# Down projection of a quantised feed-forward block: every block of sums stays in its PSUM bank and is rescaled there

## The chip, the cores and the metric

The kernel runs on one core of a Trainium2 chip. The metric is the device time of one execution in microseconds (us). Names used below: PE is TensorE (PEld its weight loads), DVE is VectorE, ACT is ScalarE, POOL is GpSimd, SP is the SyncE queue that issues most DMAs.

## The reference, cut to what matters

A gated layer: a linear attention block, whose result is added to x, and then a feed-forward block with 4-bit weights, whose result is added again. x has 32 batches of 64 rows of 512 numbers, so 2048 rows. Only the feed-forward block is touched:

```python
# per group of 128 rows of a weight matrix: w[k,n] = q[k,n]*s[g,n] - (z[g,n]+1)*s[g,n],  g = k // 128
Wg, Wu = dequant(gate...), dequant(up...)      # 512 x 1376
Wd = dequant(down...)                          # 1376 x 512: 11 groups, the last of 96 rows
gate, up = x2 @ Wg, x2 @ Wu
inter = gate * sigmoid(gate) * up              # 2048 x 1376
out = (inter @ Wd).astype(float16)
x = x + tanh(g_ffn[0]) * out
```

The weight of one group is an integer (q - z - 1, held in the tile `d_int`) times a scale that depends on the group and the output column.

## The kernel before, in words

**Stages.** The attention block works through 16 pairs of batches in a software pipeline; in its last passes the integers of the three weight matrices are unpacked into SBUF. A drain of the pipeline follows, in which the scales are transposed (`scale_T`, `d_scale_T`) and the rows are normalised for the feed-forward block. Then comes the feed-forward block, on which the change lies. It is written out as 44 units (`UNITS`): 4 chunks of 512 rows (`CHUNKS`) times 11 blocks of 128 intermediate features (`IT`). Data lie transposed: features on partitions, 512 rows along the free axis.

**One pass n of the loop over units, on PE.** Eight jobs. Each job is first `gate_up(n, job)`: two fp16 matmuls (L1395, L1396) of one weight group against the high and the low part of x, into one of three banks in turn (`gu_bank`); a job cannot start before the bank of three jobs earlier has been read. Behind it each job does one piece of the down projection of unit n-2: jobs 0 to 3 `high_product`, jobs 4 to 7 `low_product`, one for each of the four blocks of 128 output columns (`nt`), each block in a PSUM bank of its own (`z_bank`). The intermediate is split into `in_hi` and `in_lo`, so a block takes one matmul with each (L1419, L1431).

**The four blocks of the down projection differ.** Blocks 0, 1 and 2 multiply by the integers, so the sum of each unit must be multiplied by its group's scale and added to a running sum in SBUF (`yT`). Block 2 is done by DVE in one instruction (`add_sum`, L1839; L1834 for a chunk's first unit). Blocks 0 and 1 take ACT to scale (`scaled`, L880) and POOL to add (`add_sum`, L614). Block 3 (`PLAIN`) multiplies by dequantised weights, split into `wd_hi` and `wd_lo`, and its sums stay in the bank through the 11 units; it takes three matmuls for each unit (L1416, L1417, L1428), and at the chunk's end ACT copies it out (`plain_sum`). Its weights are made in the drain: a broadcast DMA (`d_scale`, L418), a POOL product (L574), an ACT copy (L833), a POOL difference (L581).

**The other engines in pass n**, in the order of their queues. DVE: the block-2 sum of unit n-3, then six `add_group` (L1800; three for gate, three for up; each scales a bank and adds it into `acc`, so the second and third of a half read what the one before wrote). ACT: `open_sum(n, 0)` (L855, first group of gate), `high_part(n-1)` (L870), `open_sum(n, 1)` (first group of up), `scaled(n-2, 0)`, `silu(n)` (L863), `scaled(n-2, 1)`, and in eight passes (`NORMALISED_IN`) one more `ffn_normalised` (L900). An up group's `add_group` needs `open_sum(n, 1)` before it. POOL: `activated(n-1)` (L592), one sum (L614), `low_part(n-1)` (L601), another sum. In chunks 1 to 3 passes 3 to 6 also transpose the finished chunk back (L1448), and DVE adds it to x (`fed_forward`, L1846). The first passes of chunks 0 and 1 carry what is left of the attention block (`LATE_UNITS`).

**The end.** After the last pass DVE takes over two POOL instructions (`last_activated`, L1810; `last_low_part`, L1818), the last two units' products follow in an order of their own (`LAST_LOWS`), and four blocks of columns are transposed (`COLUMNS`), added and stored.

Of the kernel before, what the change touches and what calls it, by code (L numbers as in the profile page):

```python
# [40 lines left out]
HIGH_ORDER = (0, 1, 3, 2)  # L41
LAST_LOWS = (3, 0, 1, 2)
COLUMNS = (3, 0, 2, 1)
# [3 lines left out]
PLAIN = slice((NJ - 1) * P, NJ * P)  # L47

# [54 lines left out]
def layer(nc, x, ctx, g_xattn, wq, wk, wv, wo, bo, g, matrices, g_ffn, out, xall, stats2, ident, w_gu, d_int,  # L103
# [5 lines left out]
    with ExitStack() as st:  # L109
# [79 lines left out]
        d_scale = sb("d_scale", [P, IT, P], F16)  # L189
# [56 lines left out]
        d_scale_in, tanh_ready = sem("d_scale_in"), sem("tanh_ready")  # L246
        d_scaled, d_hi, d_lo, ident16_made = (sem(n) for n in ("d_scaled", "d_hi", "d_lo", "ident16_made"))
        gu_mm, s0_done, acc_done, gs_ready, inter_ready, in_hi_ready, in_lo_ready = (
            sem(n) for n in ("gu_mm", "s0_done", "acc_done", "gs_ready", "inter_ready", "in_hi_ready", "in_lo_ready"))
        z_mm, z_act, z_dve, z_add, y_plain, yT_mm = (  # L250
            sem(n) for n in ("z_mm", "z_act", "z_dve", "z_add", "y_plain", "yT_mm"))
# [74 lines left out]
        def _(sp):  # L326
# [91 lines left out]
            sp.dma_start(d_scale[:, :, :], matrices[2][1][:, PLAIN].partition_broadcast(P)).then_inc(d_scale_in, 16)  # L418
# [24 lines left out]
        def _(pool):  # L443
# [123 lines left out]
            def plain_scaled():  # L567
                pool.wait_ge(f_mm, PAIRS - 1)
                pool.wait_ge(q_mm, 4 * PAIRS)
                pool.wait_ge(w_int, PAIRS - 2)  # L570
                pool.wait_ge(d_scale_in, 16)
                for its in (slice(0, IT - 1), slice(IT - 1, IT)):
                    rows = P if its.start == 0 else width(IT - 1)
                    pool.tensor_tensor(wd[0:rows, its, :], d_int[0:rows, its, PLAIN].bitcast(F32),  # L574
                                       d_scale[0:rows, its, :], ALU.mult).then_inc(d_scaled, 1)

            def plain_low():
                for part, its in enumerate((slice(0, IT - 1), slice(IT - 1, IT))):
                    rows = P if its.start == 0 else width(IT - 1)
                    pool.wait_ge(d_hi, part + 1)  # L580
                    pool.tensor_tensor(wd_lo[0:rows, its, :], wd[0:rows, its, :], wd_hi[0:rows, its, :].bitcast(F32),  # L581
                                       ALU.subtract).then_inc(d_lo, 1)

# [20 lines left out]
            def add_sum(n, nt):  # L604

                it = n % IT
                if n < 0 or it == 0 or n == UNITS - 1:
                    return
                total = yT[:, nt, :]
                pool.wait_ge(z_act, 2 * n + nt + 1)  # L610
                summed(pool, n - 1, nt)
                if it == IT - 1 and n >= IT:
                    pool.wait_ge(yT_mm, TPC * (n // IT))
                pool.tensor_tensor(yT16[:, nt, :] if it == IT - 1 else total, total, y_scaled[:, nt, :],  # L614
                                   ALU.add).then_inc(z_add, 1)

# [10 lines left out]
            plain_scaled()  # L627
# [3 lines left out]
            plain_low()  # L631
            for n in range(UNITS):
# [4 lines left out]
                add_sum(n - 3, 1)  # L637
# [24 lines left out]
        def _(act):  # L662
# [32 lines left out]
            def step(p, i, par, project, combine, residual, last=False, drain=False):  # L695
# [36 lines left out]
                if drain and combine:  # L732
# [28 lines left out]
                    plain_high()  # L761
# [67 lines left out]
            def plain_high():  # L829
                for part, its in enumerate((slice(0, IT - 1), slice(IT - 1, IT))):  # L830
                    rows = P if its.start == 0 else width(IT - 1)
                    act.wait_ge(d_scaled, part + 1)
                    act.activation(wd_hi[0:rows, its, :], wd[0:rows, its, :], ACT.Copy).then_inc(d_hi, 1)  # L833

# [37 lines left out]
            def scaled(n, nt):  # L872

                if n < 0:
                    return
                j, it = divmod(n, IT)
                act.wait_ge(z_mm, NJ * n + nt + 1)
                if n:
                    act.wait_ge(z_add, adds_done(n - 1, nt))
                act.activation(y_scaled[:, nt, :] if it else yT[:, nt, :], z_bank[nt], ACT.Copy,  # L880
                               scale=d_scale_T[:, nt, it:it + 1]).then_inc(z_act, 1)

            def plain_sum(j):

                if j == CHUNKS - 1:
# [1054 lines left out]
```

## Time and profile before

| | |
|---|---|
| time, median of 3 runs | 686.7 us (686.28 to 688.61) |
| profiled execution, first to last instruction | 684.8 us |
| busy PE / DVE / ACT / POOL | 97% / 87% / 68% / 53% |
| granted TensorE clock, mean | 0.992 |
| drain and feed-forward block | from about 390 us on; first `gate_up` at 411 us |

The time of a run covers the execution with its start and its end; the profile's span runs from the first to the last instruction, so the two differ by what lies outside, here 1.9 us against the median. A PE that is 97% busy need not be at its peak: matmuls are pipelined and a row's duration overlaps that of the next, so that the distance between two starts is what a matmul costs.

### The profile page before, as it was taken

The page shows a single profiled execution, that of the slowest core. Times are in us where ns is not written, and L with a number is a line of the kernel's source. Part 1 is how long each engine was busy: PE and PEld are TensorE (multiplying, and loading weights), DVE is VectorE, ACT ScalarE, POOL GpSimd, SP SyncE. Part 2 cuts the span into 40 slices and gives each one's busy share as a digit, 9 for nine tenths or more (in the row PEclk, how much of TensorE's full clock was granted, in tenths as well). Part 3 has the DMA queues.
Part 4 walks back from the last instruction along what each step waited for, and adds up shares of the span by engine and source line. Part 5 has one row for each costly group of instructions (what it writes and reads, how often), then busy time and mean ns, then how long its engine had stood idle before and what let it go on. Part 6 is the DMA issues. An engine that isn't in the chain of part 4 may idle for free.

```text
span 684.8 us, 14670 instructions
## 1 busy us (share of the span) xinstructions
PE 664.9 (97%) x5141; PEld 350.7 (51%) x5141; DVE 594.3 (87%) x815; ACT 468.0 (68%) x822; POOL 360.1 (53%) x434
## 2 busy tenths in 40 slices
PE   7899999999999999999999998999999999999995
PEld 6454565466455546545645533445444544454443
DVE  7777898899889889888987858999999999989987
ACT  4887677678677767767866756677665766666663
POOL 6213323223232422323236476698878877887885
PEclk8999999999999999999999999999999999999998
DMA  4122331330332122023110100000000001000102
GB/s 116 37 55 50 99 80 22 101 95 22 82 95 57 46 82 78 7 83 79 35 52 23 27 7 2 1 1 1 1 32 32 1 1 46 17 2 15 47 1 62
DMA packets 32046, 28.97 MB, mean 42 GB/s; under 512 B 20047, under 2 KB 22234, under 8 KB 32002
## 3 DMA queue, kind: packets, MB, share of 16 engines
q1 hardware_dynamic: 29594, 27.73, 14.8%
q10 hardware_dynamic: 2408, 0.70, 0.4%
q8 instruction: 22, 0.36, 0.2%
q14 instruction: 22, 0.18, 0.1%
HBM read 22.42 MB, written 4.23 MB: 39 GB/s over the span
## 4 chain that ended last, share of the span: by engine, by line
PE 86%; ACT 5%; DVE 5%; issue 1%; DMA 1%; POOL 1%; ACTq 0%; SPq 0%; DVEq 0%; POOLq 0%
PE pair L1395 8%; PE pair L1184 8%; PE small L1112 8%; PE small L1078 7%; PE pair L1396 7%; PE pair L1064 6%; ACT eq L713 4%; PE small L1096 4%; PE pair L1419 4%; PE pair L1431 4%; PE small L1395 4%; PE small L1396 4%; PE pair L1209 3%; PE pair L1043 3%; PE small L1150 3%; PE pair L1194 2%
## 5 line engine op out<-in xcount | busy, mean ns | idle before, releaser
L1800 DVE SCALAR_TENSOR_TENSOR acc<-pair,scale_T,acc 128x512 f32<-128x512 f32 (+1 forms) x176 | 131.7, 748 | 15.3 <-ACT acc L855 2.0
L614 POOL TENSOR_TENSOR yT<-yT,y_scaled 128x512 f32<-128x512 f32 (+1 forms) x78 | 100.4, 1288 | 4.6 <-ACT y_scaled L880 3.8
L704 ACT ACTIVATE ek<-pair,kneg 128x512 f32<-128x512 f32 x128 | 86.3, 682 | 18.0 <-DVE kneg L1661 18.0
L1395 PE MATMUL pair<-ek,w_gu 128*128 128x512 f16 (+1 forms) x235 | 91.3, 388 | 1.8 <-DVE acc L1800 1.4
L1396 PE MATMUL pair<-ekT,w_gu 128*128 128x512 f16 (+1 forms) x235 | 89.0, 379 | 0.0
L1666 DVE TENSOR_TENSOR eq<-eq,pair 128x1024 f32<-128x1024 f32 x64 | 77.8, 1216 | 11.2 <-PE pair L1169 11.0
L1656 DVE TENSOR_REDUCE qmax<-pair 128x16 f32<-128x1024 f32 x64 | 78.2, 1222 | 8.5 <-PE pair L1043 7.6
L1661 DVE TENSOR_REDUCE kneg<-pair 128x2 f32<-128x1024 f32 x64 | 77.9, 1218 | 0.9 <-PE pair L1064 0.6
L1419 PE MATMUL pair<-in_hi,d_int 128*128 128x512 f32 (+1 forms) x132 | 75.8, 575 | 1.3 <-DVE yT L1839 1.3
L592 POOL TENSOR_TENSOR inter<-act_gate,acc 128x512 f32<-128x512 f32 (+1 forms) x43 | 55.1, 1281 | 40.5 <-DVE acc L1800 16.7
L713 ACT ACTIVATE eq<-pair 128x1024 f32<-128x1024 f32 x64 | 65.8, 1028 | 15.2 <-PE pair L1194 15.1
L1431 PE MATMUL pair<-in_lo,d_int 128*128 128x512 f32 (+1 forms) x132 | 75.4, 573 | 0.0
L1800 DVE SCALAR_TENSOR_TENSOR acc<-small,scale_T,acc 128x512 f32<-128x512 f32 (+1 forms) x88 | 65.8, 748 | 8.5 <-ACT acc L855 1.9
L460 POOL TENSOR_TENSOR rn_sq<-ss_max,minus_half 128x8 f32<-128x8 f32 x16 | 26.4, 1650 | 82.5 <-DVE ss_max L1599 82.5
L709 ACT ACTIVATE ekT<-pair 128x1024 f32<-128x1024 f32 x64 | 65.4, 1022 | 4.5 <-PE pair L1209 4.5
L86 POOL TENSOR_TENSOR ln_work<-stats 128x2 f32<-128x2 f32 (+4 forms) x34 | 6.6, 194 | 115.1 <-DVE stats L1508 113.6
L870 ACT ACTIVATE in_hi<-inter 128x512 fp32r<-128x512 f32 (+1 forms) x44 | 27.8, 631 | 54.7 <-POOL inter L592 54.3
L1112 PE MATMUL small<-ekT,ctxT 128*64 128x512 f32 x256 | 64.6, 605 | 0.0
L601 POOL TENSOR_TENSOR in_lo<-inter,in_hi 128x512 fp32r<-128x512 f32 (+1 forms) x43 | 55.2, 1284 | 4.4 <-ACT in_hi L870 4.4
L1078 PE MATMUL small<-eq,fold 128*64 128x512 f32 x240 | 57.1, 598 | 0.0
L880 ACT ACTIVATE y_scaled<-pair,d_scale_T 128x512 f32<-128x512 f32 x78 | 53.2, 682 | 2.2 <-PE pair L1431 1.3
L855 ACT ACTIVATE acc<-pair,scale_T 128x512 f32<-128x512 f32 (+1 forms) x59 | 40.5, 686 | 20.8 <-PE pair L1396 20.8
(205 smaller groups left out, 1463.9 us busy)
## 6 DMA issues: line engine op xcount, KB each, us to landing
xall<-in_x SPq DMA_DIRECT2D x16, 256.0 KB, 2.8
ctx_raw<-in_ctx SPq DMA_DIRECT2D x16, 256.0 KB, 3.0
out_x<-xall SPq DMA_DIRECT2D x16, 256.0 KB, 2.0
zero<-zeros_plus SPq DMA_DIRECT2D x8, 344.0 KB, 5.3
packed<-in_L_ffn_gate_qweight SPq DMA_DIRECT2D x4, 688.0 KB
packed<-in_L_ffn_up_qweight SPq DMA_DIRECT2D x4, 688.0 KB
packed<-in_L_ffn_down_qweight SPq DMA_DIRECT2D x10, 256.0 KB
zero<-zeros_plus SPq DMA_DIRECT2D x5, 256.0 KB, 4.9
```

The lines of the kernel that those rows point to most:

```text
L614: pool.tensor_tensor(yT16[:, nt, :] if it == IT - 1 else total, total, y_scaled[:, nt, :], ALU.add).then_inc(z_add, 1)
L704: act.activation(ek[:, b, t, :], k_pairs[t % 2][:, b, :], ACT.Exp, bias=kneg[:, b, t:t + 1], scale=-1.0, accum_out=ksum[:, k_slot(b, t):k_ ...
L713: act.activation(eq[:, par, t, :, :], k_pair[:, :, :], ACT.Exp).then_inc(q_exp, 1)
L1078: last = pe.matmul(small[1][half(b), :], fold[:, k_slot(b, t), :], eq[:, par, t, b, :], start=(t == 0), stop=(t == OT - 1))
L1112: last = pe.matmul(small[0][half(b), :].rearrange("c (t e d) -> c t e d", t=OT, e=2), ctxT[:, t, half(b)], heads, start=(t == 0), stop=(t ...
L1395: pe.matmul(gu_bank[count % 3][0:w, :], lhsT, xT_hi[:, g, rows], start=True, stop=False)
L1396: pe.matmul(gu_bank[count % 3][0:w, :], lhsT, xT_lo[:, g, rows], start=False, stop=True).then_inc(gu_mm, 1)
L1419: pe.matmul(z_bank[nt], d_int[0:w, it, nt * P:(nt + 1) * P], in_hi[0:w, n % 2, :], start=True, stop=False)
L1431: pe.matmul(z_bank[nt], d_int[0:w, it, nt * P:(nt + 1) * P], in_lo[0:w, n % 2, :], start=False, stop=True).then_inc(z_mm, 1)
L1656: dve.tensor_reduce(qmax[:, t, :, 0:HEADS], dve_pair[:, :, :].rearrange("n b (h d) -> n b h d", d=DH), AX.X, ALU.max).then_inc(t_max, 1)
L1661: dve.tensor_reduce(kneg[:, :, t], k_pairs[t % 2][:, :, :], AX.X, ALU.min).then_inc(k_max, 1)
L1800: dve.scalar_tensor_tensor(out=acc[0:w, n % 2, m, :], in0=gu_bank[(8 * n + job) % 3][0:w, :], scalar=scale_T[0:w, it, 4 * m + g:4 * m + g ...
```

## The change

Block 3 is treated like the others: integer weights, two matmuls for each unit. No block is evacuated per unit any more. The sums stay in the PSUM banks, and before the next unit's products are added, the bank is multiplied in place by the ratio of this group's scale to the next one's, s[g] / s[g+1] (`rescale`); at a chunk's last unit it is multiplied by the last scale on its way to `yT16`. ACT does this for blocks 0, 1 and 3, DVE for block 2; at the end of the kernel DVE takes block 3 of unit 42 and blocks 0 and 2 of unit 43. POOL adds nothing any more, and the making of block 3's weights goes. DVE computes the ratios once, in four instructions in pass 1 (`rescale_factors`). The low products follow the order of the high ones (`BANKS`), and the last columns are done in another order.

```diff
-HIGH_ORDER = (0, 1, 3, 2)
+BANKS = (0, 1, 3, 2)
+ACT_BANKS = (0, 1, 3)
 LAST_LOWS = (3, 0, 1, 2)
-COLUMNS = (3, 0, 2, 1)
+COLUMNS = (3, 0, 1, 2)
...
+def bank_products(n, nt):
+
+    return NJ * n + (LAST_LOWS if n == UNITS - 1 else BANKS).index(nt) + 1
...
         def summed(eng, n, nt):
 
-            if nt == 2:
+            last = n - UNITS + 2
+            if last >= 0 and nt in ((3, 2), (0, 2))[last]:
+                eng.wait_ge(z_dve, UNITS - 2 + 2 * last + ((3, 2), (0, 2))[last].index(nt) + 1)
+            elif last >= 0:
+                eng.wait_ge(z_act, 3 * (UNITS - 2) + 2 * last + ((0, 1), (3, 1))[last].index(nt) + 1)
+            elif nt == 2:
                 eng.wait_ge(z_dve, n + 1)
-            elif n % IT:
-                eng.wait_ge(z_add, adds_done(n, nt))
             else:
-                eng.wait_ge(z_act, 2 * n + nt + 1)
+                eng.wait_ge(z_act, 3 * n + ACT_BANKS.index(nt) + 1)
...
-            sp.dma_start(d_scale[:, :, :], matrices[2][1][:, PLAIN].partition_broadcast(P)).then_inc(d_scale_in, 16)
...
             sp.wait_ge(columns_out, 2)
+            store_columns(1)
+            sp.wait_ge(columns_out, 3)
             store_columns(2)
-            sp.wait_ge(columns_out, 3)
-            store_columns(1)
...
-            plain_scaled()
             ffn_normalised(6)
             step(PAIRS, 0, True, False)
             ffn_normalised(7)
-            plain_low()
             for n in range(UNITS):
...
-                add_sum(n - 3, 1)
...
-                add_sum(n - 2, 0)
-            add_sum(UNITS - 3, 1)
             pool.wait_ge(inter_ready, UNITS)
-            add_sum(UNITS - 2, 0)
-            add_sum(UNITS - 2, 1)
...
                     transposed(3)
-                    plain_high()
                     transposed(4)
...
-            def scaled(n, nt):
+            def bank_scaled(n, nt):
...
                 j, it = divmod(n, IT)
...
+                act.wait_ge(z_mm, bank_products(n, nt))
+                if n == 0:
+                    act.wait_ge(rescale_ready, 1)
+                if it < IT - 1:
+                    act.activation(z_bank[nt], z_bank[nt], ACT.Copy, scale=rescale[:, nt, it:it + 1]).then_inc(z_act, 1)
+                    return
                 if j:
                     act.wait_ge(yT_mm, TPC * j)
-                act.activation(yT16[:, NJ - 1, :], z_bank[NJ - 1], ACT.Copy).then_inc(y_plain, 1)
+                act.activation(yT16[:, nt, :], z_bank[nt], ACT.Copy, scale=d_factor[:, nt, it:it + 1]).then_inc(z_act, 1)
...
-                scaled(n - 2, 0)
+                bank_scaled(n - 2, 0)
                 silu(n)
...
-                scaled(n - 2, 1)
-                if n > IT and n % IT == 1:
-                    plain_sum(n // IT - 1)
+                bank_scaled(n - 2, 1)
+                bank_scaled(n - 2, 3)
                 if n in NORMALISED_IN:
                     ffn_normalised(NORMALISED_IN.index(n) + 2 * TPC)
-            scaled(UNITS - 2, 0)
+            bank_scaled(UNITS - 2, 0)
             high_part(UNITS - 1)
-            scaled(UNITS - 2, 1)
-            plain_sum(CHUNKS - 1)
+            bank_scaled(UNITS - 2, 1)
+            bank_scaled(UNITS - 1, 3)
+            bank_scaled(UNITS - 1, 1)
...
-                elif n and nt == 2:
-                    pe.wait_ge(z_dve, n)
-                elif n and nt < 2:
-                    pe.wait_ge(z_act, 2 * (n - 1) + nt + 1)
-                elif it == 0 and j:
-                    pe.wait_ge(y_plain, j)
-                if nt == NJ - 1:
-                    if n == 0:
-                        pe.wait_ge(d_lo, 2)
-                    pe.matmul(z_bank[nt], wd_hi[0:w, it, :], in_hi[0:w, n % 2, :], start=it == 0, stop=False)
-                    pe.matmul(z_bank[nt], wd_lo[0:w, it, :], in_hi[0:w, n % 2, :], start=False, stop=False)
-                else:
-                    pe.matmul(z_bank[nt], d_int[0:w, it, nt * P:(nt + 1) * P], in_hi[0:w, n % 2, :], start=True, stop=False)
+                elif n:
+                    summed(pe, n - 1, nt)
+                pe.matmul(z_bank[nt], d_int[0:w, it, nt * P:(nt + 1) * P], in_hi[0:w, n % 2, :], start=it == 0, stop=False,
+                          skip_group_check=True)
...
+                pe.matmul(z_bank[nt], d_int[0:w, it, nt * P:(nt + 1) * P], in_lo[0:w, n % 2, :], start=False,
+                          stop=True, skip_group_check=True).then_inc(z_mm, 1)
...
-                        low_product(n - 2, job - NJ)
+                        low_product(n - 2, BANKS[job - NJ])
...
+            def rescale_factors():
+
+                dve.wait_ge(sT_ready, 2)
+                dve.tensor_scalar(d_inverse[:, :, :], d_scale_T[:, :, :], 0.0, NO_SCALE, ALU.is_equal,
+                                  ALU.mult).then_inc(factor_step, 1)
+                dve.wait_ge(factor_step, 1)
+                dve.tensor_tensor(d_factor[:, :, :], d_scale_T[:, :, :], d_inverse[:, :, :], ALU.add).then_inc(factor_step, 1)
+                dve.wait_ge(factor_step, 2)
+                dve.reciprocal(d_inverse[:, :, :], d_factor[:, :, :]).then_inc(factor_step, 1)
+                dve.wait_ge(factor_step, 3)
+                dve.tensor_tensor(rescale[:, :, :], d_factor[:, :, 0:IT - 1], d_inverse[:, :, 1:IT],
+                                  ALU.mult).then_inc(rescale_ready, 1)
+
+            def bank_scaled(n, nt):
...
+                dve.wait_ge(z_mm, bank_products(n, nt))
+                if n == 0:
+                    dve.wait_ge(rescale_ready, 1)
+                if it < IT - 1:
+                    dve.tensor_scalar(z_bank[nt], z_bank[nt], rescale[:, nt, it:it + 1], None, ALU.mult).then_inc(z_dve, 1)
                     return
...
+                dve.tensor_scalar(yT16[:, nt, :], z_bank[nt], d_factor[:, nt, it:it + 1], None, ALU.mult).then_inc(z_dve, 1)
...
-                add_sum(n - 3, 2)
+                bank_scaled(n - 3, 2)
+                if n == 1:
+                    rescale_factors()
...
             last_activated()
-            add_sum(UNITS - 3, 2)
+            bank_scaled(UNITS - 3, 2)
+            bank_scaled(UNITS - 2, 3)
             last_low_part()
-            add_sum(UNITS - 2, 2)
-            add_sum(UNITS - 1, 0)
-            add_sum(UNITS - 1, 2)
+            bank_scaled(UNITS - 2, 2)
+            bank_scaled(UNITS - 1, 0)
+            bank_scaled(UNITS - 1, 2)
             last_columns(0)
-            add_sum(UNITS - 1, 1)
+            last_columns(1)
             last_columns(2)
-            last_columns(1)
```

Tiles that nothing uses any more (`wd`, `wd_hi`, `wd_lo`, `d_scale`, `yT`, `y_scaled`) and their semaphores go as well.

## Rows read from the trace of the kernel before

**Rows 1.** Windows view, 525 to 550 us: busy time (x instructions) by engine, clock, DMA.

```profile
core 0: us, PE busy (x) PEld busy (x) DVE busy (x) ACT busy (x) POOL busy (x), PEclk, DMA share, GB/s
...
525.00:550.00 25.00, 25.00 (x118) 13.51 (x117) 22.77 (x33) 18.01 (x31) 21.62 (x18) 1.00 0.00 1
```

**Rows 2.** Timeline of PE, first matmuls of jobs 2, 3 and 6: start, duration, instruction.

```profile
503.36 0.38 PE L1395 MATMUL small<-ek,w_gu 128*128 128x512 f16 x1
...
504.26 0.39 PE L1395 MATMUL pair<-ek,w_gu 128*128 128x512 f16 x1
...
506.30 0.39 PE L1395 MATMUL pair<-ek,w_gu 128*128 128x512 f16 x1
```

**Rows 3.** Groups by line on DVE, 424.6 to 672.2 us: busy, mean ns, idle before.

```profile
L1800 DVE SCALAR_TENSOR_TENSOR acc<-pair,scale_T,acc 128x512 f32<-128x512 f32 (+1 forms) x168 | 125.7, 748 | 13.9 <-ACT acc L855 1.0 <-DVE acc L1800 0.5
L1800 DVE SCALAR_TENSOR_TENSOR acc<-small,scale_T,acc 128x512 f32<-128x512 f32 (+1 forms) x84 | 62.8, 748 | 7.9 <-ACT acc L855 1.9
```

**Rows 4.** Timeline of DVE and ACT, 602 to 615 us, one plain unit.

```profile
609.00 0.74 DVE L1839 SCALAR_TENSOR_TENSOR yT<-pair,d_scale_T,yT 128x512 f32<-128x512 f32 x1
...
609.66 0.74 DVE L1800 SCALAR_TENSOR_TENSOR acc<-pair,scale_T,acc 128x512 f32<-128x512 f32 x1
...
610.51 0.75 DVE L1800 SCALAR_TENSOR_TENSOR acc<-small,scale_T,acc 128x512 f32<-128x512 f32 x1
...
611.36 0.75 DVE L1800 SCALAR_TENSOR_TENSOR acc<-pair,scale_T,acc 128x512 f32<-128x512 f32 x1
611.54 0.69 ACT L855 ACTIVATE acc<-pair,scale_T 128x512 f32<-128x512 f32 x1 [0.37 <-PE pair L1396]
...
612.33 0.75 DVE L1800 SCALAR_TENSOR_TENSOR acc<-small,scale_T,acc 128x512 f32<-128x512 f32 x1 [0.22 <-ACT acc L855]
...
613.22 0.69 ACT L880 ACTIVATE y_scaled<-pair,d_scale_T 128x512 f32<-128x512 f32 x1
...
614.26 0.69 ACT L855 ACTIVATE acc<-small,scale_T 128x512 f32<-128x512 f32 x1 [0.35 <-PE small L1396]
...
614.71 0.74 DVE L1839 SCALAR_TENSOR_TENSOR yT<-pair,d_scale_T,yT 128x512 f32<-128x512 f32 x1
```

**Rows 5.** The page's costliest groups: POOL's sums.

```profile
L614 POOL TENSOR_TENSOR yT<-yT,y_scaled 128x512 f32<-128x512 f32 (+1 forms) x78 | 100.4, 1288 | 4.6 <-ACT y_scaled L880 3.8
```

**Rows 6.** Timeline of ACT and DVE where pass 13 ends and pass 14 begins.

```profile
495.92 0.82 ACT L900 ACTIVATE xn_more<-xall,ln_work 128x512 f32<-128x512 f32 x1
...
496.63 0.69 ACT L855 ACTIVATE acc<-pair,scale_T 128x512 f32<-128x512 f32 x1
...
497.50 0.74 DVE L1800 SCALAR_TENSOR_TENSOR acc<-small,scale_T,acc 128x512 f32<-128x512 f32 x1
```

**Rows 7.** Timelines of DVE, ACT and POOL, 384 to 437 us: drain and first passes.

```profile
396.88 0.55 DVE L1670 RECIPROCAL rden<-den_sq 128x64 f32<-128x64 f32 x1 [4.67 <-DMA den_sq<-den]
...
419.38 1.60 DVE L1800 SCALAR_TENSOR_TENSOR acc<-pair,scale_T,acc 128x512 f32<-128x512 f32 x2
...
425.43 0.75 DVE L1800 SCALAR_TENSOR_TENSOR acc<-small,scale_T,acc 128x512 f32<-128x512 f32 x1 [0.83 <-ACT acc L855]
...
436.61 0.16 DVE L1599 TENSOR_SCALAR ss_max<-ss_sq 128x8 f32<-128x8 f32 x1
...
409.20 0.60 ACT L826 ACTIVATE ek<-pair 128x512 f16<-128x512 f32 x1 [0.89 <-PE pair L993]
...
412.58 3.32 POOL L581 TENSOR_TENSOR wd_lo<-wd,wd_hi 128x1280 fp32r<-128x1280 f32 x2
418.95 1.27 POOL L592 TENSOR_TENSOR inter<-act_gate,acc 128x512 f32<-128x512 f32 x1 [3.04 <-DVE acc L1800]
```

**Rows 8.** Timelines of two stretches: an uncontended DVE product, and the kernel's end.

```profile
385.11 0.68 DVE L1593 TENSOR_TENSOR d_int<-packed,zero 96x512 fp32r<-96x512 int32 x1
...
671.16 2.53 POOL L614 TENSOR_TENSOR yT<-yT,y_scaled 128x512 f32<-128x512 f32 x2
...
672.95 1.30 DVE L1810 TENSOR_TENSOR inter<-act_gate,acc 96x512 f32<-96x512 f32 x1
...
674.94 1.21 DVE L1818 TENSOR_TENSOR in_lo<-inter,in_hi 96x512 fp32r<-96x512 f32 x1
...
680.48 0.75 DVE L1851 SCALAR_TENSOR_TENSOR xall<-pair,tanh_ffn,xall 128x512 f32<-128x512 f16 x1
```

More of the change, by code:

```diff
@@ L40 @@
 XSCALE = 256.0
-HIGH_ORDER = (0, 1, 3, 2)
+BANKS = (0, 1, 3, 2)
+ACT_BANKS = (0, 1, 3)
 LAST_LOWS = (3, 0, 1, 2)
-COLUMNS = (3, 0, 2, 1)
+COLUMNS = (3, 0, 1, 2)
+NO_SCALE = 1e-20
 LATE_UNITS = (2, 4, 7, 9, 11, 18, 20, 22)
@@ L143, in layer @@
         d_scale_T = sb("d_scale_T", [P, NJ, IT])
+        d_factor = sb("d_factor", [P, NJ, IT])
+        d_inverse = sb("d_inverse", [P, NJ, IT])
+        rescale = sb("rescale", [P, NJ, IT - 1])
         with ExitStack() as attention_only:
@@ L565, in late_residual @@
                 pool.tensor_tensor(xall[:, k, :], xall[:, k, :], yn[:, :], ALU.add).then_inc(x1_done, 1)
[L567 to L582, printed above, removed]
             def activated(n):
@@ L602, in low_part @@
                                    ALU.subtract).then_inc(in_lo_ready, 1)
[L604 to L615, printed above, removed]
             second_moments(0)
@@ L827, in transposed @@
                                ACT.Copy).then_inc(xT_hi_ready, 1)
[L829 to L833, printed above, removed]
             step(0, 0, 0, True, False, False)
@@ L1426, in low_product @@
                     pe.wait_ge(in_lo_ready, n + 1)
-                if nt == NJ - 1:
-                    pe.matmul(z_bank[nt], wd_hi[0:w, it, :], in_lo[0:w, n % 2, :], start=False,
-                              stop=it == IT - 1).then_inc(z_mm, 1)
-                else:
-                    pe.matmul(z_bank[nt], d_int[0:w, it, nt * P:(nt + 1) * P], in_lo[0:w, n % 2, :], start=False,
-                              stop=True).then_inc(z_mm, 1)
+                pe.matmul(z_bank[nt], d_int[0:w, it, nt * P:(nt + 1) * P], in_lo[0:w, n % 2, :], start=False,
+                          stop=True, skip_group_check=True).then_inc(z_mm, 1)
             def rows_transposed(j, t):
@@ L1442, in rows_transposed @@
                     pe.wait_ge(xT_lo_ready, PAIRS)
-                for nt in (0, 3, 2, 1):
-                    if t == 0 and nt == NJ - 1:
-                        pe.wait_ge(y_plain, j + 1)
-                    elif t == 0:
+                for nt in BANKS:
+                    if t == 0:
                         summed(pe, IT * j + IT - 1, nt)
@@ L1454, in columns_transposed @@
                     pe.wait_ge(out_ready, PAIRS - TPC)
[L1455 removed]
                 else:
                     pe.wait_ge(acc_done, 6 * UNITS)
[L1458 removed]
+                summed(pe, UNITS - 1, nt)
                 for t in range(TPC):
@@ L1480, in _ @@
                     if n >= 2 and job < NJ:
-                        high_product(n - 2, HIGH_ORDER[job])
+                        high_product(n - 2, BANKS[job])
                     elif n >= 2:
-                        low_product(n - 2, job - NJ)
+                        low_product(n - 2, BANKS[job - NJ])
                     if n <= LATE_UNITS[-1]:
@@ L1825, in add_sum @@
                 j, it = divmod(n, IT)
-                total, scale = yT[:, nt, :], d_scale_T[:, nt, it:it + 1]
-                if n == UNITS - 1:
-                    dve.wait_ge(z_mm, NJ * n + LAST_LOWS.index(nt) + 1)
-                else:
-                    dve.wait_ge(z_mm, NJ * n + (NJ if n == UNITS - 2 else nt + 1))
-                if it == 0:
-                    if n:
-                        dve.wait_ge(z_dve, n)
-                    dve.tensor_scalar(total, z_bank[nt], scale, None, ALU.mult).then_inc(z_dve, 1)
+                dve.wait_ge(z_mm, bank_products(n, nt))
[3 more added lines that the diff above has]
+                    dve.tensor_scalar(z_bank[nt], z_bank[nt], rescale[:, nt, it:it + 1], None, ALU.mult).then_inc(z_dve, 1)
                     return
-                summed(dve, n - 1, nt)
-                if it == IT - 1 and j:
+                if j:
                     dve.wait_ge(yT_mm, TPC * j)
-                dve.scalar_tensor_tensor(out=yT16[:, nt, :] if it == IT - 1 else total, in0=z_bank[nt], scalar=scale,
-                                         in1=total, op0=ALU.mult, op1=ALU.add).then_inc(z_dve, 1)
+                dve.tensor_scalar(yT16[:, nt, :], z_bank[nt], d_factor[:, nt, it:it + 1], None, ALU.mult).then_inc(z_dve, 1)
             def fed_forward(j, t):
```

29 lines of the change are left out of this document (3 added, 26 removed).

## The prediction

> **What bounds the kernel now.** I read the page first, then windows of the feed-forward block, then the timeline of single units, then the groups by line on DVE, and last the drain and the end. All that the change touches in bulk lies behind 411 us, in 44 units.
>
> The window shows PE busy in all of its 25 us, DVE 22.77, POOL 21.62 and ACT 18.01 [rows 1]. That reads like a PE bound, and the change takes a matmul from each unit. But a busy PE is a modelled end, so the starts must be looked at. A job with three matmuls takes 0.68 us (from 504.26 three jobs on to 506.30), the job with four 0.90 [rows 2]. So a matmul costs 0.22, and a unit on PE costs 7 x 0.68 + 0.90 = 5.66 us where nothing holds it.
>
> Now DVE in a plain unit [rows 4]. It starts the block-2 sum at 609.00 and the next one at 614.71: 5.71. Inside, 0.66 passes from that sum to the first add; two adds that depend on one another stand 0.85 apart (609.66, 610.51, 611.36), though each lasts 0.75. The fourth starts 0.97 behind the third, because it waits for ACT's `open_sum` (611.54), which waits for PE; without that it would start 0.66 behind. So DVE's own minimum is about 5.71 - 0.31 = 5.40. The reader is to see that DVE stands only 0.26 below PE, and that its 91% in the window is nearly all it can give: the gaps of 0.10 between dependent adds count as idle and cannot be filled in this order.
>
> The groups by line put a number on what DVE could still give back [rows 3]: 13.9 + 7.9 = 21.8 us idle before its 252 adds between 424.6 and 672.2 us. Two adds of three depend on the one before: 168 x 0.10 = 16.8. What is left, 5.0 us in 247, is all of its real waiting. Where units carry more DVE work (the late attention pieces, `fed_forward`) DVE waits for nobody.
>
> **The change part by part.**
>
> *PE, 44 matmuls fewer.* 44 x 0.22 = 9.7 us on PE alone; a unit becomes 8 x 0.68 = 5.44. That is still just above DVE's 5.40, so the two engines are level and the gain ends where DVE stands. Of the 5.0 us, 0.83 at 425.43 is a wait for ACT behind attention leftovers [rows 7] and stays. Of the other 4.2 I leave 1.2 for the 0.04 by which PE is still longer in some twenty plain units and for handovers of two level engines. Gain 3.0; bounds 1.5 (half the waiting stays) and 4.2.
>
> *DVE's block-2 instruction* stays one of the same length class: it read a bank and wrote SBUF, now it reads and writes the bank. No row shows an engine other than PE writing a bank. The nearest rows for what the memory of an operand can do are ACT's: 0.82 with a source in SBUF, 0.69 with one in a bank [rows 6], 0.13 apart. So the bound is 44 x 0.13 = 5.7 us of loss, on the engine that sets the pace. The other way nothing is to be had, for PE's 5.44 stands next. I take 0, since within DVE a scaled sum and an add from banks take 0.74 and 0.75 [rows 4], whatever their other operands.
>
> *POOL, 78 sums of 1.29 fewer* [rows 5], 100 us of busy time. POOL is not on the path: where it is late, its product waits for DVE's add. Worth nothing in the units themselves; it pays at the end (below).
>
> *ACT, a third scaled bank in each pass.* Two instructions of this kind follow one another by less than their length: 0.82 long, the next 0.71 later [rows 6], so 0.69 long means 0.58 more in the queue. Behind it stands `open_sum(n+1, 0)`, for which DVE's first add and with it PE's bank wait. In a plain unit ACT idles 0.35 before that instruction [rows 4], so this cover does not hold all of it. The loop decides: from `open_sum(n, 1)` to the next `open_sum` ACT now needs 2.72 - 0.35 + 0.58 = 2.95; from there through 0.69 on ACT, an add of 0.75 and a job of 0.68 to the next `open_sum(n, 1)` about 2.1. Sum 5.1, below 5.40: it fits. Not so in the seven passes from 3 on with `ffn_normalised`: 0.71 more makes 5.8, 0.4 too much. In pass 13 the slack is small already: `open_sum` ends at 497.32 and DVE's add starts at 497.50 [rows 6]. Upper bound 7 x 0.4 = 2.8; lower bound 0, since in most of these passes DVE carries late attention work too and is itself longer. I take +0.8.
>
> *`rescale_factors`.* Four dependent DVE instructions on 128x44 in pass 1. Rows of such size run from 0.16 (8 columns) to 0.55 (a reciprocal of 64) [rows 7]; between these by columns about 0.2, 0.2, 0.4 and 0.2, and handovers: +1.1, bounds 0.6 and 2.2. DVE has no idle before the adds of pass 1 (419.38) [rows 7], and ACT, POOL and PE all wait for those adds, so this lies on the path in full.
>
> *Drain.* The broadcast DMA, two steps on POOL (the second 3.32 us) and the ACT copies go. All are covered: POOL ends `plain_low` at 415.90 and then idles 3.04 us until DVE's add; ACT waits 0.89 for PE behind its copies [rows 7]. Nothing.
>
> *The end.* `last_activated` takes 1.30 and `last_low_part` 1.21 on DVE; a product of the same 96x512 from SBUF with POOL idle takes 0.68 [rows 8]. POOL's last sums run beside both, and go: 0.62 + 0.53 = 1.15 gained, in line with the last products. Ahead of `last_low_part` comes one more bank of 0.66, mostly while ACT makes `in_hi`; behind it DVE loses one of its last instructions to ACT (block 1 of the last unit), 0.66. Net -1.3; bounds -1.8 and 0.
>
> **Sum:** -3.0 + 0.8 + 1.1 - 1.3 = -2.4 us on the profiled span of 684.8, so 682.4. The median of the runs lies 1.9 above the span; that part stays: 684.3.
>
> **Rivals.**
>
> *PE was the bound after all.* Then the whole 9.7 comes off: about 677. For it: PE's full window, and plain units of 5.71 against its 5.66. Against it: DVE's 5.40 and its 5.0 us of real waiting. Chance 0.04.
>
> *ACT's queue takes the place.* The third bank delays `open_sum` in the normalised passes at full price, and the sum becomes -2.4 + 2.0 = -0.4: 686.3. For it: slack of 0.18 in pass 13. Against it: the loop of 5.1, and PE's shorter jobs let `open_sum(n, 1)` start earlier. Chance 0.23.
>
> *Writing a bank is dearer for DVE (slower than before).* Place: `bank_scaled` on DVE, 44 times. From 2.4 / 44 = 0.055 us each the gain is gone, from 0.10 the kernel is slower by more than 0.3%, at the bound of 0.13 it takes 684.3 + 5.7 = 690.0. For it: ACT's rows show that memory can matter by that much; against it: DVE's rows for banks show one length. Chance 0.13. The Trainium skill, "VectorE: DVE Perf Modes", section on the TRN2 errata, gives a fixed cost of 120 cycles for an instruction from PSUM and 58 from SBUF at 0.96 GHz; if a bank as destination cost the same difference, an estimate of 0.065 us each and 2.8 us in all, the time would be about 687.1. No row here shows such a destination, so the rule lends this rival its chance and no more.
>
> My forecast has 0.55, the remaining 0.05 goes to an unforeseen stall of either size.
>
> **How the numbers follow.** A measurement of this kernel tells some 0.3%, or 2.1 us, from no change. The forecast's own range is 681.3 (all terms at their good bounds: -4.2 + 0.6 - 1.8 = -5.4) to 686.5. The range given, 681.0 to 688.2, takes in the ACT rival and the cheap half of the bank rival, and leaves out PE's and the dear half: under 2 in 10. Faster by over 0.3% (below 684.6): 0.40 of the forecast, 0.04 from PE, 0.04 from ACT, 0.02 elsewhere, 0.50. Slower (above 688.8): 0.09 from the bank rival, 0.03 from ACT, 0.03 from the rest, 0.15. Between: 0.35.
>
> **What would show it.** In the profile after: plain units 5.4 to 5.5 us apart on DVE and units with `fed_forward` unchanged; the waits of DVE's adds on ACT down from 5.0 us to 2 or less; PE's rows waiting on DVE's adds more often than now; POOL some 100 us less busy; `last_activated` near 0.7. Wrong if DVE's in-place row is longer than 0.80 or the distance behind it longer than 0.66; if the first add of a unit waits for `open_sum` in passes without `ffn_normalised`; if PE's high products wait for a rescaled bank; or if `rescale_factors` is hidden.

## The result and the profile after

| | before | after |
|---|---|---|
| time, median | 686.83 us (686.11 to 688.65, 20 runs) | 688.66 us (687.32 to 692.59, 20 runs) |
| profiled span | 684.8 us | 687.2 us |
| busy DVE / ACT / POOL | 594.3 / 468.0 / 360.1 us | 594.6 / 488.2 / 257.3 us |

The ratio is 1.0023, 95% interval 1.0013 to 1.0033: the kernel became slower by 1.8 us. The forecast was 684.3, with a range up to 688.2, so the time lies 0.5 us above the range and on the other side of the old time. The profiled run of the kernel after took 689.25 us, 0.6 above its median; readings of its trace therefore add up to the 2.4 us between the two spans and not to 1.8.

The change did in bulk what it says. The windows view of the kernel after, in the stretch of [rows 1]:

```profile
core 0: us, PE busy (x) PEld busy (x) DVE busy (x) ACT busy (x) POOL busy (x), PEclk, DMA share, GB/s
525.00:550.00 25.00, 24.90 (x111) 12.23 (x110) 22.61 (x33) 19.45 (x33) 10.47 (x9) 1.00 0.02 5
```

PE issues 111 matmuls where it issued 118, POOL is busy half as long, ACT 1.4 us more. DVE, which sets the pace in plain units as the last experiment below shows, is as busy as before.

A plain unit on DVE and ACT, timeline of the kernel after, the unit that answers to [rows 4]:

```profile
613.04 0.75 DVE L1775 TENSOR_SCALAR pair<-pair,rescale 128x512 f32<-128x512 f32 x1
613.70 0.74 DVE L1732 SCALAR_TENSOR_TENSOR acc<-pair,scale_T,acc 128x512 f32<-128x512 f32 x1
...
615.39 0.75 DVE L1732 SCALAR_TENSOR_TENSOR acc<-pair,scale_T,acc 128x512 f32<-128x512 f32 x1
616.18 0.75 DVE L1732 SCALAR_TENSOR_TENSOR acc<-small,scale_T,acc 128x512 f32<-128x512 f32 x1
...
618.56 0.75 DVE L1775 TENSOR_SCALAR pair<-pair,rescale 128x512 f32<-128x512 f32 x1
...
615.39 0.69 ACT L809 ACTIVATE acc<-pair,scale_T 128x512 f32<-128x512 f32 x1 [0.20 <-PE pair L1344]
615.98 0.65 ACT L835 ACTIVATE pair<-pair,rescale 128x512 f32<-128x512 f32 x1
```

Three things are to be seen. The bank written in place costs DVE the same 0.75, and the next add follows it by 0.66 as before. The fourth add stands 0.79 behind the third (616.18 after 615.39) where it stood 0.97 before and could stand 0.66. The unit takes 5.52 (613.04 to 618.56) instead of 5.71.

Then the place where the time went. DVE and POOL in passes 0 and 1 of the kernel after, answering to [rows 7]:

```profile
419.35 0.88 DVE L1756 TENSOR_SCALAR d_inverse<-d_scale_T 128x44 f32<-128x44 f32 x1
420.27 0.20 DVE L1759 TENSOR_TENSOR d_factor<-d_scale_T,d_inverse 128x44 f32<-128x44 f32 x1
420.51 0.43 DVE L1761 RECIPROCAL d_inverse<-d_factor 128x44 f32<-128x44 f32 x1
420.97 1.28 DVE L1763 TENSOR_TENSOR rescale<-d_factor,d_inverse 128x40 f32<-128x40 f32 x1
422.17 1.59 DVE L1732 SCALAR_TENSOR_TENSOR acc<-pair,scale_T,acc 128x512 f32<-128x512 f32 x2
...
418.93 1.27 POOL L573 TENSOR_TENSOR inter<-act_gate,acc 128x512 f32<-128x512 f32 x1 [6.33 <-DVE acc L1732]
420.93 1.26 POOL L582 TENSOR_TENSOR in_lo<-inter,in_hi 128x512 fp32r<-128x512 f32 x1 [0.74 <-ACT in_hi L824]
```

Two of the four instructions are long, and both end when a POOL instruction ends: the first at 420.23, POOL's product at 420.20; the last at 422.25, POOL's difference at 422.19. The add that began at 419.38 before [rows 7] begins at 422.17. PE stands still meanwhile, and the windows view of the same kernel shows what follows:

```profile
417.00:420.00 3.00, 1.97 (x8) 0.42 (x6) 3.00 (x5) 0.69 (x1) 1.07 (x1) 1.00 0.00 0
420.00:423.00 3.00, 0.03 (x1) 0.03 (x2) 2.81 (x5) 0.63 (x1) 2.26 (x3) 0.79 0.00 0
423.00:426.00 3.00, 2.78 (x7) 0.60 (x8) 2.67 (x4) 1.63 (x3) 0.42 (x1) 0.50 0.00 0
426.00:429.00 3.00, 3.00 (x10) 1.12 (x8) 1.55 (x3) 2.23 (x4) 1.10 (x1) 0.57 0.03 5
429.00:432.00 3.00, 3.00 (x21) 1.36 (x20) 2.21 (x3) 1.20 (x2) 1.45 (x2) 1.00 0.00 0
```

The columns are those of [rows 1]; PEclk is the third from the right. PE did 0.03 us of work in 420 to 423, the granted clock went to 0.50, the level of 1.2 GHz, and was back at 1.00 from 429 on. PE's timeline shows it in single matmuls:

```profile
419.49 0.38 PE L1344 MATMUL small<-ekT,w_gu 128*128 128x512 f16 x1
422.97 0.61 PE L1343 MATMUL pair<-ek,w_gu 128*128 128x512 f16 x1 [3.10 <-DVE acc L1732]
...
428.99 0.39 PE L1343 MATMUL pair<-ek,w_gu 128*128 128x512 f16 x1
```

In what follows a distance of a unit is that from the start of its first add on DVE's timeline to the next unit's. From the first unit's to the second's it was 6.76 before and is 9.58; the next two distances went from 6.05 to 6.78 and from 5.84 to 6.46. Together 4.17 us more.

The groups by line on DVE, 428 to 675 us, answer to [rows 3]:

```profile
L1732 DVE SCALAR_TENSOR_TENSOR acc<-pair,scale_T,acc 128x512 f32<-128x512 f32 (+1 forms) x167 | 124.7, 748 | 13.8 <-ACT acc L809 1.7 <-PE pair L1344 0.2
L1732 DVE SCALAR_TENSOR_TENSOR acc<-small,scale_T,acc 128x512 f32<-128x512 f32 (+1 forms) x84 | 62.9, 748 | 8.1 <-PE small L1344 1.2 <-ACT acc L809 1.1
L1775 DVE TENSOR_SCALAR pair<-pair,rescale 128x512 f32<-128x512 f32 x38 | 28.5, 749 | 0.0
```

Idle time is 21.9 us, no less than the 21.8 before. But 2.1 of it are three waits of 1.19, 0.20 and 0.71 at 428.95, 430.76 and 432.22, at the slow clock or just behind it; without these, and without the 0.83 at 425.43 before, 21.0 became 19.8. By the prediction's own working 167 x 0.10 of this is the spacing of dependent adds, so some 3.1 us of real waiting are left, where 2 or less was to show that it was right.

### The profile page after: what moved, and what is told of

It reads as the page before. It is cut to its first block, busy times and chain, and to the rows that moved or that the text cites. A ratio compares the mean times of both kernels' runs of the same rounds, so it can differ in the third digit from the quotient of the medians.

```text
span 687.2 us, 14346 instructions
## 1 busy us (share of the span) xinstructions
PE 665.2 (97%) x5097; PEld 342.9 (50%) x5097; DVE 594.6 (87%) x819; ACT 488.2 (71%) x860; POOL 257.3 (37%) x352
## 4 chain that ended last, share of the span: by engine, by line
PE 85%; DVE 5%; ACT 4%; issue 1%; DMA 1%; SPq 1%; POOL 1%; DVEq 0%; POOLq 0%
PE pair L1343 9%; PE pair L1132 8%; PE small L1060 8%; PE pair L1344 7%; PE small L1026 6%; PE pair L1357 6%; PE pair L1366 6%; PE pair L1012 6%; PE small L1343 4%; PE small L1044 4%; ACT eq L674 4%; PE pair L1157 4%; PE small L1344 4%; PE small L1098 3%; PE pair L991 3%; PE pair L1142 2%
## 5 line engine op out<-in xcount | busy, mean ns | idle before, releaser
L1357 PE MATMUL pair<-in_hi,d_int 128*128 128x512 f32 (+1 forms) x176 | 101.0, 577 | 0.7 <-DVE pair L1775 0.6
L1366 PE MATMUL pair<-in_lo,d_int 128*128 128x512 f32 (+1 forms) x176 | 100.3, 574 | 0.0
L835 ACT ACTIVATE pair<-pair,rescale 128x512 f32<-128x512 f32 x119 | 74.9, 658 | 0.8 <-PE pair L1366 0.8
L1343 PEld LDWEIGHTS pair<-ek,w_gu 128*128 128x128 bf16 (+1 forms) x235 | 23.2, 99 | 67.1 <-DVE acc L1732 42.6
```

Source lines behind the costliest of these rows:

```text
L1343: pe.matmul(gu_bank[count % 3][0:w, :], lhsT, xT_hi[:, g, rows], start=True, stop=False)
L1357: pe.matmul(z_bank[nt], d_int[0:w, it, nt * P:(nt + 1) * P], in_hi[0:w, n % 2, :], start=it == 0, stop=False, skip_group_check=True)
L1366: pe.matmul(z_bank[nt], d_int[0:w, it, nt * P:(nt + 1) * P], in_lo[0:w, n % 2, :], start=False, stop=True, skip_group_check=True).then_inc ...
```

## Experiments

All ratios are to the kernel before, run on the same chip. It took 687.23 us beside the experiments with the factors in the drain, the factors alone, PE kept busy and the normalisation on POOL, and 686.82 beside the other three. Where times from these two sets, or from one of them and the result, are compared, the difference of the ratios is given too.

### The four instructions earlier

After, with `rescale_factors` called between two steps of the drain instead of in pass 1:

```diff
+                    rescale_factors()
                     normalise(2)
...
-                if n == 1:
-                    rescale_factors()
```

> The changed kernel, with the four DVE instructions of rescale_factors moved from pass 1 into the drain, where DVE waits 0.96 us for PE and POOL is idle. Theory (the loss is made in passes 0 to 2 alone: 2.8 us by these four instructions, two of which stand still until a POOL product of two SBUF tiles has ended, and 1.35 us by the lower TensorE clock behind PE's idle 3.1 us): each of the four takes 0.2 to 0.45, the clock stays at 1.00, the time falls by about 4.1 us to 684.6, 2.2 below the kernel before. Rival 1 (scaling in the banks is dearer for DVE or ACT over all 44 units): nothing changes, 688.7. Rival 2 (the four instructions cost their own length wherever they stand): 1.1 us stays, 685.7.

Measured: 684.46 us, ratio 0.9958 (0.9946 to 0.9970). DVE's timeline of this kernel:

```profile
405.74 0.18 DVE L1578 TENSOR_SCALAR d_inverse<-d_scale_T 128x44 f32<-128x44 f32 x1
405.95 0.21 DVE L1581 TENSOR_TENSOR d_factor<-d_scale_T,d_inverse 128x44 f32<-128x44 f32 x1
406.19 0.43 DVE L1583 RECIPROCAL d_inverse<-d_factor 128x44 f32<-128x44 f32 x1
406.66 0.20 DVE L1585 TENSOR_TENSOR rescale<-d_factor,d_inverse 128x40 f32<-128x40 f32 x1
406.80 1.22 DVE L1611 TENSOR_TENSOR eq<-eq,pair 128x1024 f32<-128x1024 f32 x1
```

The same instructions take 0.18, 0.21, 0.43 and 0.20 with POOL idle, and the step behind them starts at 406.80 against 406.79 in the kernel after: they fill a hole in which DVE waited 0.96 for PE. The first three distances are 6.40, 6.05 and 5.74. So everything that the kernel after lost hangs on the place of these four instructions. The first distance is also 0.36 below the 6.76 of the kernel before; what gave that is not known.

### The four instructions alone

Before, with the same four instructions in pass 1, whose results nobody reads:

```diff
+                if n == 1:
+                    rescale_factors()
```

> The kernel before, with nothing of the change but the four instructions of rescale_factors at the same place in pass 1; nobody uses their result. Theory: all of the 4.1 us comes back, 690.9, with two of the four instructions at 0.9 and 1.3 us and the clock at half behind them. Rival (they cost what the prediction gave them): 1.1 us, 687.9. Rival (the loss belongs to the banks): no change, 686.8.

Measured: 690.93 us, ratio 1.0057 (1.0041 to 1.0073), 3.7 us more than the 687.23 of the kernel before beside it. The rows of `d_inverse`, first and last instruction, by duration (ns, least, median, most) and start:

```profile
L1651 DVE TENSOR_SCALAR d_inverse<-d_scale_T x1: 882/882/882, 419.1 to 419.1; 128x44 f32<-128x44 f32 x1
L1658 DVE TENSOR_TENSOR rescale<-d_factor,d_inverse x1: 1278/1278/1278, 420.7 to 420.7; 128x40 f32<-128x40 f32 x1
```

The first three distances are 9.58, 6.99 and 6.81, and the granted clock is 0.50 from 423 to 429 us. The loss comes without any of the rest of the change.

### PE kept busy through the hole

After, with twelve matmuls into an unused bank while PE would stand still:

```diff
+                    if n == 1 and job == GH:
+                        pe.wait_ge(xT_lo_ready, 6)
+                        for _ in range(12):
+                            pe.matmul(z_bank[1], w_gu[:, 0, 0, 0:P], xT_hi[:, 0, 0:CHUNK], start=True, stop=True)
```

> The changed kernel, with twelve matmuls of 512 columns into an unused bank on PE in pass 1, just where PE otherwise idles 3.1 us for DVE; their result is overwritten. Theory (passes 1 and 2 are 0.7 and 0.6 longer because the granted clock falls to 0.50 after the idle): the clock stays at 1.00, PE's fp16 rows there last 0.39 and not 0.61, and the time falls by about 1.3 us to 687.4. Rival (these passes are longer because ACT's and POOL's work queued up behind the late adds): clock 1.00 and no gain, 688.7.

Measured: 687.30 us, ratio 1.0002 (0.9993 to 1.0011), 1.4 us less than the kernel after, by the times and by the ratios. Its windows:

```profile
420.00:423.00 3.00, 2.41 (x11) 0.72 (x9) 2.86 (x4) 0.24 (x2) 2.49 (x2) 1.00 0.00 0
423.00:426.00 3.00, 2.18 (x10) 0.84 (x11) 2.79 (x6) 2.25 (x4) 0.00 (x0) 1.00 0.00 0
426.00:429.00 3.00, 3.00 (x21) 1.32 (x20) 2.06 (x3) 2.10 (x4) 1.38 (x2) 1.00 0.02 5
```

The clock stays at 1.00 and the second and third distances fall from 6.78 and 6.46 to 6.05 and 5.74, while the first stays at 9.59. So the clock is a part of the price by itself: 0.73 + 0.72 against this run. Against the kernel before it is 0.73 + 0.62 = 1.35 us, since the third distance gains some 0.1 from the matmul that goes (5.84 became 5.72 in the experiment on the matmul below).

### POOL held back

After, with POOL's first product made to wait for the ratios, so that POOL is idle beside the four instructions:

```diff
+                if n == 0:
+                    pool.wait_ge(rescale_ready, 1)
```

> The changed kernel, rescale_factors still in pass 1, but POOL's first product waits until they are done, so that POOL is idle beside them. Theory (the first and the last of the four stand still until a POOL product of two SBUF tiles ends): they take 0.2, 0.2, 0.43 and 0.2, pass 0 lasts 7.9 instead of 9.6, and since PE then idles 1.4 and not 3.1 us its clock may stay at 1.00: 685.6, or 687 if the clock falls all the same. Rival (the two are long by themselves at this place): 0.9 and 1.3 again, and POOL's work comes later by 3 us on top: 688.7 or more.

Measured: 686.35 us, ratio 0.9994 (0.9985 to 1.0002), less than the kernel after by 2.3 us by the times and 2.0 by the ratios. DVE's and PE's timelines and the windows of this kernel:

```profile
418.54 0.17 DVE L1758 TENSOR_SCALAR d_inverse<-d_scale_T 128x44 f32<-128x44 f32 x1
...
419.45 0.20 DVE L1765 TENSOR_TENSOR rescale<-d_factor,d_inverse 128x40 f32<-128x40 f32 x1
...
420.37 0.39 PE L1345 MATMUL pair<-ek,w_gu 128*128 128x512 f16 x1 [1.31 <-DVE acc L1734]
...
422.48 0.61 PE L1345 MATMUL small<-ek,w_gu 128*128 128x512 f16 x1 [0.65 <-DVE acc L1734]
```

```profile
420.00:423.00 3.00, 1.73 (x6) 0.48 (x7) 2.88 (x5) 1.75 (x4) 2.26 (x2) 0.90 0.00 0
423.00:426.00 3.00, 3.00 (x10) 1.12 (x8) 1.69 (x3) 2.62 (x5) 2.04 (x3) 0.53 0.02 5
```

In the place where they took 2.8 us the four instructions now take 1.03 (first distance 7.79 against 6.76 before). That shows POOL as the cause of the length. The clock did not stay at 1.00: PE's longest wait is 1.31, the clock still went down, and the second and third distances, 6.72 and 6.47, are as long as in the kernel after. The time lies between the two that were expected, 685.6 and 687.

### A matmul fewer in the kernel before

To measure the first term of the sum alone: before, without one of block 3's three matmuls, that of `wd_lo` with `in_hi`; the low part of these weights is left out of the sums.

```diff
-                    pe.matmul(z_bank[nt], wd_lo[0:w, it, :], in_hi[0:w, n % 2, :], start=False, stop=False)
```

> The kernel before, without the second of block 3's three matmuls (wd_lo with in_hi; the low part of these weights is left out of the sum): 44 matmuls fewer and nothing else of the change. Theory (DVE sets the pace, PE stands 0.26 us above it only in plain units): what the changed kernel gained from pass 24 on, 1.8 us, comes off, 685.0; with the 3.0 of the prediction it would be 683.8. Rival (PE is the bound): 44 x 0.22 = 9.7 us, 677.1.

Measured: 685.36 us, ratio 0.9975 (0.9965 to 0.9985), 1.5 us less by the medians, 1.0 to 2.4 by the interval. The plain units come to the same lengths as in the kernel after (5.40, 5.39, 5.65, 5.44, 5.52). So the gain of the change in the units is that of the matmul, and it is about half of what was forecast.

### The normalisation moved to POOL

The kernel of the first experiment, with the eight late `ffn_normalised` on POOL, which now has room, instead of ACT:

```diff
+                if n in NORMALISED_IN:
+                    late_normalised(NORMALISED_IN.index(n) + 2 * TPC)
...
-                if n in NORMALISED_IN:
-                    ffn_normalised(NORMALISED_IN.index(n) + 2 * TPC)
```

> As the run with the factors in the drain, and the eight late ffn_normalised move from ACT to POOL, which has been idle for most of each pass since its sums went. Theory (behind the third scaled bank, ACT's 0.7 us of ffn_normalised makes the next open_sum late and DVE's first add with it: +0.25, +0.27, +0.25 and +0.18 in passes 8, 13, 19 and 21): these go, and some of ACT's delay of 0.8 ahead of pass 2: 1.0 to 1.7 us less than that run, about 683.3. Rival (the first add waits for something else, or POOL's 2.1 us make the product late on which in_hi and the second open_sum hang): same as that run or slower, 684.6 or more.

Measured: 682.99 us, ratio 0.9943 (0.9931 to 0.9956): the fastest version that leaves nothing out, ahead of both kernels. The distances of passes 3, 8, 13, 19 and 21 went from 6.25, 6.25, 5.77, 6.25 and 6.16 to 6.08, 6.00, 5.39, 6.00 and 5.99, together 1.2 us of the 1.5 by which the two versions differ. On POOL the instruction takes longer, as this row of its timeline shows (ACT: 0.83), but DVE's adds do not wait for it:

```profile
493.47 2.08 POOL L553 TENSOR_SCALAR xn_more<-xall,ln_work 128x512 f32<-128x512 f32 x1
```

The part of the expectation on the first passes missed: 5.35 + 6.60 stand there for 6.05 + 5.74, which is 0.16 more.

### One more matmul out

The kernel just above, without the high product of block 1 in all units but a chunk's first; these products are left out of the sums:

```diff
-                pe.matmul(z_bank[nt], d_int[0:w, it, nt * P:(nt + 1) * P], in_hi[0:w, n % 2, :], start=it == 0, stop=False,
-                          skip_group_check=True)
+                if nt != 1 or it == 0:
+                    pe.matmul(z_bank[nt], d_int[0:w, it, nt * P:(nt + 1) * P], in_hi[0:w, n % 2, :], start=it == 0, stop=False,
+                              skip_group_check=True)
```

> The run with the factors in the drain and the late ffn_normalised on POOL, without block 1's high product in all units but the first of each chunk (left out of the sums): 40 matmuls fewer again. Theory (DVE sets the pace): plain units go from 5.39 to 5.64 down to DVE's 5.40 and stop there, about 1 us off the 683.0. Rival (PE still sets it): 40 x 0.22 = 8.8 us, 674.2.

Measured: 681.89 us, ratio 0.9933 (0.9921 to 0.9946). For 40 matmuls of 0.22 that is 1.1 us less than the kernel it builds on by the times, 0.7 by the ratios, whose intervals overlap, and 0.8 in the eleven plain units from unit 24 on of the two profiles. Its window:

```profile
525.00:550.00 25.00, 24.29 (x109) 11.66 (x106) 22.64 (x33) 18.93 (x33) 15.39 (x11) 1.00 0.00 1
```

PE is now less than full, DVE's 33 instructions take the same 22.64, and plain units stand at 5.38 to 5.42 but for one of 5.65. DVE's own order of instructions is the bound there, PE is not.

## Why the prediction was wrong

**The step that failed is the cost of `rescale_factors`,** put at +1.1 us with bounds of 0.6 and 2.2. It measured 4.17. The working took durations of similar instructions from rows that no POOL instruction made longer, and for an idle POOL it was right: with POOL held back the four cost 1.03. What it left out came in two parts. The first is POOL: the first and last of the four wait for a running POOL instruction, 0.88 for 0.18 and 1.28 for 0.20, 1.8 us. The second is what the hole does to PE: the granted clock falls to 1.2 GHz, 1.35 us. 1.03 + 1.8 + 1.35 = 4.2. The rows for the first part were on the table: the prediction read from [rows 8] that `last_activated` and `last_low_part` take 1.30 and 1.21 beside POOL and 0.68 without, and used it for the end of the kernel only. That a POOL product runs at 418.95 to 420.22, just where the first of the four was to stand, is in [rows 7]; the next one, from 420.96 on, is in the same trace. No rival named either part; both fell into the 0.05 left for an unforeseen stall.

The Trainium skill, "SBUF — State Buffer", section "Who interferes with whom", states the first part: a DVE instruction with two inputs in SBUF, or one of the kinds that may use both read ports on a single input (`tensor_scalar` among them), uses ports that it shares with GpSimd, and whichever is second waits for the whole instruction of the other. The traces agree instruction by instruction: the `tensor_scalar` and the last product waited to POOL's end, the first product (420.27), also of two SBUF tiles, met an idle POOL and took 0.20, and two adds with one input from a bank took 1.59 together (422.17) beside the next POOL instruction (422.15 to 423.41), as they took 1.60 in [rows 7]. The prediction did not draw on it.

Two rows on which the prediction leant say more than it read from them, as POOL's timeline of the kernel before shows:

```profile
385.14 0.72 POOL L464 TENSOR_TENSOR rn_parts<-rn_sq,rn_parts 128x8 fp32r<-128x8 f32 x1
395.98 4.19 POOL L555 TENSOR_SCALAR xn_more<-xall,ln_work 128x512 f32<-128x512 f32 x2
410.21 0.21 POOL L464 TENSOR_TENSOR rn_parts<-rn_sq,rn_parts 128x8 fp32r<-128x8 f32 x1
```

The DVE product at 385.11 in [rows 8] was not uncontended. It came first, took its 0.68, and it was POOL's small product, begun 0.03 later, that lasted 0.72 in place of 0.21. And the reciprocal at 396.88 in [rows 7], with one input, ran beside a POOL instruction without growing: it takes the same 0.55 at 373.93, where POOL is idle.

**PE, 44 matmuls fewer: −3.0 forecast, −1.8 measured.** Right in its mechanism, too large in size. The eleven plain units from unit 24 on took 62.2 us and take 60.4; the experiment on the matmul alone gives −1.5. The floor of DVE was read rightly: five of the eleven stand at 5.39 to 5.41, and the units with `fed_forward` stayed at 6.05. But there are eleven plain units, not some twenty, and the other six are 0.13 to 0.25 longer, as at 616.18, where DVE waits for ACT's `open_sum`, which had waited 0.20 for PE. The remaining waits of two level engines were put too low, and the number of units too high.

**ACT's third bank: +0.8 forecast, +1.05.** Right in place, and near in price. Timeline of ACT and DVE in pass 13, kernel after, as in [rows 6]:

```profile
500.77 0.83 ACT L848 ACTIVATE xn_more<-xall,ln_work 128x512 f32<-128x512 f32 x1
501.48 0.70 ACT L809 ACTIVATE acc<-pair,scale_T 128x512 f32<-128x512 f32 x1
502.28 0.75 DVE L1732 SCALAR_TENSOR_TENSOR acc<-small,scale_T,acc 128x512 f32<-128x512 f32 x1 [0.28 <-ACT acc L809]
```

The slack of 0.18 has become a wait of 0.28. Passes 3, 8, 13, 19 and 21 grew by 0.10, 0.25, 0.27, 0.25 and 0.18; in the other normalised passes DVE's own work covers it, as the lower bound supposed. In plain units the loop fits.

**Writing a bank: 0 forecast, 0 measured.** DVE's in-place instruction takes 749 ns, `add_sum` (L1839) took 742 before, and the next starts 0.66 later; ACT's takes 658, from this row of the page after, where the instruction it replaces (`scaled`, L880 before) took 682 to SBUF:

```profile
L835 ACT ACTIVATE pair<-pair,rescale 128x512 f32<-128x512 f32 x119 | 74.9, 658 | 0.8 <-PE pair L1366 0.8
```

The rival of a dearer bank is refuted, and with it the estimate of 0.065 us each that the prediction worked out from the Trainium skill, "VectorE: DVE Perf Modes", section on the TRN2 errata. The Trainium skill, "ScalarE: Activation LUTs", section "Step-by-step: what each stage is for", has ScalarE faster into PSUM than into SBUF; the 24 ns agree.

**Drain: nothing forecast, nothing seen.** The first add stands at 412.59 against 412.61. In the profiles of the experiments it stands anywhere from 411.7 to 412.6, so less than about 0.9 could not be told there.

**The end: −1.3 forecast, −0.67.** Timeline of DVE and SP at the end of the kernel after, as in [rows 8]:

```profile
675.97 0.69 DVE L1742 TENSOR_TENSOR inter<-act_gate,acc 96x512 f32<-96x512 f32 x1
677.90 0.68 DVE L1750 TENSOR_TENSOR in_lo<-inter,in_hi 96x512 fp32r<-96x512 f32 x1
681.53 2.65 SPq L426 DMA_DIRECT2D out_x<-xall  x4
682.08 0.74 DVE L1790 SCALAR_TENSOR_TENSOR xall<-small,tanh_ffn,xall 128x512 f32<-128x512 f16 x1
```

Both products take 0.69 and 0.68 as forecast, and DVE's last instruction comes 1.4 us earlier behind the first of them than before (6.11 against 7.53). But from the first add of the last unit to the end it is 16.26 against 16.92. The first of the four stores is issued only 0.8 earlier (5.56 behind `last_activated` against 6.32), and the end follows it by 5.65 us, against 5.52 before. The DMA view, 678 to 688 us of the kernel after in 40 slices, shows why that may be:

```profile
GB/s 0 0 0 0 0 0 0 0 0 0 0 0 0 33 0 0 0 10 276 287 293 183 166 264 307 289 273 281 315 275 293 293 293 99 0 0 0 0 0 0
out_x<-xall SPq DMA_DIRECT2D x4, 256.0 KB, 2.6
```

From the first store on the four of 256 KB move almost without a gap, at some 280 GB/s, so the end follows the first store and not the last product. This is read from the trace; no run tried it.

**The sum.** 4.17 − 1.83 + 1.05 − 0.67 = +2.7; a wait of 0.36 in unit 16, which the kernel before and the experiment on the matmul show (6.41 and 6.40) and all other profiles do not (6.05), takes it to +2.4, and the spans differ by 2.4. What makes that wait is not known. With 4.17 for 1.1 alone the forecast would have been 687.4, inside its range; the units and the end, each short of its gain, make the rest. With the four instructions in a hole the kernel takes 684.46, close to the 684.3 forecast, but that is luck: there they cost nothing where 1.1 was charged, and the units and the end gave less.

**The range** was drawn too narrow above. Its lower end adds up all terms at their good bounds. The same sum at the bad bounds, -1.5 + 2.8 + 2.2 and 0, gives +3.5 on the 686.7 of the kernel before, 690.2 and not 686.5, and the measured 688.66 lies below that, though the term that failed lies beyond its own bound of 2.2.

**Rivals.** PE as the bound is refuted by the two experiments that take matmuls out: 9.7 us less work on PE brought 1.5, and 8.8 more brought about 1. ACT's queue took its place at the forecast's price and not at the rival's.

## What to carry to other kernels

Before a few small instructions are put on the path, look at what the neighbours do in the same microseconds: here a DVE instruction with two SBUF tiles, or a `tensor_scalar` within SBUF, did not end before the POOL product it met, however small it was. A stall ahead of PE can be paid twice, when the clock falls behind it, so one-time work belongs in a hole where its engine waits anyway. When the full engine stands a few per cent above the next one, relieving it is worth only that distance, and the number of units that show it must be counted.

## What the runs showed of the hardware

- DVE and POOL held each other up for whole instructions, and the second to come waited. DVE beside a POOL product: 0.88 in place of 0.18 us (`tensor_scalar`, 128x44 in SBUF), 1.28 in place of 0.20 (product, 128x40), 1.30 and 1.21 in place of 0.69 and 0.68 (products, 96x512). POOL beside a DVE product: 0.72 in place of 0.21. A reciprocal with one input in SBUF (0.55) and adds with one of two inputs in a bank (0.75) were not held up.
- A stall of PE cost more than its length: 3.10 us of idle were followed by 5.5 us (422.97 to 428.50) of fp16 matmuls of 0.61 to 0.65 in place of 0.38, at a granted clock of 0.50, the 1.2 GHz level. With POOL held back no wait was longer than 1.31, and the clock fell all the same, for some 3 us. Twelve matmuls without use in the hole kept it at 1.00.
- PSUM as source and destination of one instruction was hardly dearer than PSUM to SBUF on DVE, 749 ns against 742, with the next instruction 0.66 us behind either, and cheaper on ACT, 658 against 682.
